# TensorE's step reordered: the transposes of quad 3 and of h ahead of the first feed-forward product, P V ahead of the first values

## What is computed

```python
x = x + tanh(g_xattn) * xattn(layernorm(x), ctx, dist, ...)   # 4 layers
x = x + tanh(g_ffn)   * ffn(layernorm(x), ...)                # 1 layer
# in each layer of xattn, norm(x) = (x - mean) / (std + 1e-6):
q, k, v = norm(x) @ Wq * 64**-0.5, ctx @ Wk, ctx @ Wv         # 16 heads of 64
bias = relu(dist[..., None] @ Wth + bth) @ Wto + bto + mask   # 32 hidden units
w = softmax(q k^T + bias)
x = x + (w v) @ Wo
x = x + relu(norm(x) @ Wf1 + bf1) @ Wf2 + bf2                 # 512 hidden units
```

## Time and profile before

| | us |
|---|---|
| median of 3 runs | 1382.73 |
| lowest, highest | 1380.3, 1384.69 |
| the profiled execution's own time | 1388.81 |
| its span in the profile | 1387.1 |
| PE busy | 1228.3 (89%) |
| DVE busy | 1222.8 (88%) |
| ACT busy | 1064.8 (77%) |
| POOL busy | 834.8 (60%) |

### The profile page before, as it was taken

One profiled execution on the slowest core, in us unless ns is written; L12 is line 12 of the kernel. 1 busy time (PEld: TensorE's weight loads), 2 busy tenths in 40 slices (PEclk: granted clock), 3 DMA queues, 4 the chain that ended last, 5 costly groups with the idle time before them and its releaser, 6 DMA issues.

```text
span 1387.1 us, 39817 instructions
## 1 busy us (share of the span) xinstructions
PE 1228.3 (89%) x11184; PEld 1013.8 (73%) x11184; DVE 1222.8 (88%) x4922; ACT 1064.8 (77%) x3353; POOL 834.8 (60%) x889
## 2 busy tenths in 40 slices
PE   1599989898989899898989898989898999788897
PEld 1377878787878787777878787878787878666665
DVE  4899989898989999898989898989898988579996
ACT  4588878787878888787878686878787876568886
POOL 3677767676767677676767676767676754211110
PEclk9899999999999999999999999999999999989999
DMA  5201000002110000021100101111101000000000
GB/s 153 67 7 30 16 27 12 29 12 76 44 31 12 23 19 22 20 68 34 31 25 13 29 12 31 57 47 28 31 12 42 12 12 9 5 22 19 18 20 9
DMA packets 69117, 41.06 MB, mean 30 GB/s; under 512 B 14841, under 2 KB 63873, under 8 KB 68993
## 3 DMA queue, kind: packets, MB, share of 16 engines
q1 hardware_dynamic: 68992, 39.84, 10.1%
HBM read 23.29 MB, written 1.05 MB: 18 GB/s over the span
## 4 chain that ended last, share of the span: by engine, by line
issue 27%; DVE 24%; ACT 18%; PE 17%; POOL 3%; DVEq 1%; DMA 1%; ACTq 0%; SPq 0%; POOLq 0%
ACT prob L802 10%; DVE bias_acc L951 4%; PE M L582 3%; ACT relu_z L785 3%; PE O L552 3%; DVE score L998 3%; DVE qT L1123 3%; DVE hid L1073 3%; DVE st L1016 2%; PE M L628 2%; PE M L560 2%; PE L L689 1%; ACT probT L809 1%; ACT oT L814 1%; DVE rs L1025 1%
## 5 line engine op out<-in xcount | busy, mean ns | idle before, releaser
L802 ACT ACTIVATE prob<-score,nmax 128x128 f32<-128x128 f32 x1024 | 396.7, 390 | 182.7 <-DVE nmax L998 177.3
L1396 POOL TENSOR_TENSOR prob<-prob,rinv 128x512 f32<-128x512 f32 x256 | 293.9, 1148 | 234.0 <-DVE rinv L1006 231.9
L951 DVE SCALAR_TENSOR_TENSOR bias_acc<-relu_z,cst,bias_acc 128x512 f32<-128x512 f32 x370 | 339.7, 918 | 9.7 <-ACT relu_z L785 0.2
L785 ACT ACTIVATE relu_z<-dist_g,cst 128x512 f32<-128x512 f32 x386 | 294.9, 804 | 16.9 <-DMA cst<-cst_all 16.9
L998 DVE CUSTOM_DVE_ANT_0 score<-L,bias 128x128 f32<-128x128 f32 x1024 | 233.8, 282 | 4.2 <-PE L L528 1.5
L802 ACT ACTIVATION_READ_ACCUMULATOR prob<-score,nmax 128x1 f32 x1024 | 193.2, 189 | 0.0
L1391 POOL TENSOR_TENSOR sd<-mv,half 128x1 f32<-128x1 f32 x128 | 105.6, 825 | 120.4 <-DVE mv L1018 117.6
L538 PE MATMUL T<-ident,prob 128*128 128x128 f32 x1024 | 163.9, 284 | 4.7 <-POOL prob L1396 3.8
L552 PEld LDWEIGHTS O<-probT,v 128*64 128x64 f32 x2048 | 109.3, 136 | 62.0 <-issue 54.4
L582 PE MATMUL M<-wv,ctxT 128*128 128x512 f32 x256 | 147.0, 658 | 7.7 <-DVE hid L1073 5.1
L528 PE MATMUL L<-kT,qT 64*128 64x128 f32 x2048 | 149.6, 286 | 0.0
(11 more groups left out here) (134 smaller groups left out, 2226.7 us busy)
## 6 DMA issues: line engine op xcount, KB each, us to landing
dist_g<-in_fside_BxSxS SPq DMA_DIRECT2D x16, 256.0 KB, 2.7
mask_g<-in_mask_Bx1x1xS_ff SPq DMA_DIRECT2D x16, 256.0 KB, 3.5
ctxT<-ctxT_all SPq DMA_DIRECT2D x64, 64.0 KB, 1.9
xs<-x_all SPq DMA_DIRECT2D x64, 64.0 KB, 1.8
x_all<-xs SPq DMA_DIRECT2D x64, 64.0 KB, 1.9
wk<-in_L_xattn_Wk SPq DMA_DIRECT2D x4, 512.0 KB, 3.7
wv<-in_L_xattn_Wv SPq DMA_DIRECT2D x4, 512.0 KB, 4.3
wq<-in_L_xattn_Wq SPq DMA_DIRECT2D x4, 512.0 KB, 5.0
```

What stands on the lines that cost most here:

```text
L785: nc.scalar.activation(relu_z[:, z_slot(g, k), :], dist_g[:, :, :], ACT.Relu, bias=cst[:, C_BTH + k:C_BTH + k + 1], scale=cst[:, C_WTH + k ...
L802: last = nc.scalar.activation(prob[:, c, m, :], score[:, c, m, :], ACT.Exp, bias=nmax[:, c, m:m + 1], scale=-1.0, accum_out=rsum[:, c, m:m ...
L951: vec.scalar_tensor_tensor(out=bias_acc[:, :], in0=relu_z[:, z_slot(g, k), :], scalar=weight, in1=bias_acc[:, :], op0=ALU.mult, op1=ALU.ad ...
L1396: gp.tensor_tensor(prob[:, c, :, :], prob[:, c, :, :], rinv[:, c, :].rearrange("p (m o) -> p m o", o=1).broadcast_to([P, 4, P]), ALU.mult) ...
```

## The change

Each engine's step is edited where it has to follow PE's new order.

- PE: after the first scores come now the transpose of quad 3 of unit i-1 and the transpose of h of unit i+1, and then the first feed-forward product of unit i-2. Later in the step the second half of P V of unit i-1 comes ahead of the first values product.
- DVE: the copies probT (quad 3) and hT come ahead of the relu hid.
- ACT: the exponentials of quad 1 come ahead of the copy of the first values.
- POOL and SP are not edited. No instruction is added or taken out on any engine.

```diff
@@ PE, step @@
                 if cur:
                     scores(g, i, 0)
+                if prev:
+                    turn(g, i - 1, 3)
+                if nxt:
+                    pe.wait_ge(h_done[0], after(g, i + 1, 1))
+                    wait(pe, h2T_kept, after(g, i - 2, 1))
+                    nc.tensor.transpose(M2[:, 0:P], h[:, (i + 1) % 2, :], ident[:, :]).then_inc(hT_done, 1)
                 if old:
 
                     pe.wait_ge(h2T_kept, after(g, i - 2, 1))
...
                     for c in range(FILT // P):
                         last = mm(M1[:, c * P:(c + 1) * P], wf1[:, c * P:(c + 1) * P], h2T[:, i % 2, :], start=True, stop=True)
                     last.then_inc(f1_done, 1)
-
-                if prev:
-                    turn(g, i - 1, 3)
-                if nxt:
-                    pe.wait_ge(h_done[0], after(g, i + 1, 1))
-                    wait(pe, h2T_kept, after(g, i - 2, 1))
-                    nc.tensor.transpose(M2[:, 0:P], h[:, (i + 1) % 2, :], ident[:, :]).then_inc(hT_done, 1)
+                if nxt:
                     keys(g, i + 1, 1)
+                if prev:
+                    apply(g, i - 1, 1)
+                if nxt:
                     values(g, i + 1, 0)
-                if prev:
-                    apply(g, i - 1, 1)
@@ ACT, step @@
                 relus(g, i, 1)
+                if cur:
+                    exps(g, i, 1)
                 if nxt:
                     act.wait_ge(v_done, after(g, i + 1, 2, 0))
                     wait(act, pv_done, after(g, i - 1, 2, 1))
                     nc.scalar.activation(v[:, (i + 1) % 2, 0:512], M1[:, :], copy).then_inc(v_kept[0], 1)
-                if cur:
-                    exps(g, i, 1)
@@ DVE, step @@
                 if cur:
                     score_quad(g, i, 0)
+                if prev:
+                    keep_turned(g, i - 1, 3)
+                if nxt:
+                    dve.wait_ge(hT_done, after(g, i + 1, 1))
+                    wait(dve, q_done, after(g, i - 1, 2, 1))
+                    vec.tensor_copy(hT[:, (i + 1) % 2, :], M2[:, 0:P]).then_inc(hT_kept, 1)
                 if old:
 
                     for c in range(FILT // P):
...
                     last.then_inc(hid_kept, 1)
-
-                if prev:
-                    keep_turned(g, i - 1, 3)
-                if nxt:
-                    dve.wait_ge(hT_done, after(g, i + 1, 1))
-                    wait(dve, q_done, after(g, i - 1, 2, 1))
-                    vec.tensor_copy(hT[:, (i + 1) % 2, :], M2[:, 0:P]).then_inc(hT_kept, 1)
```

More of the change, by code:

```diff
@@ L629, in step @@
                     last.then_inc(f1_done, 1)
-                if prev:
-                    turn(g, i - 1, 3)
                 if nxt:
-                    pe.wait_ge(h_done[0], after(g, i + 1, 1))
-                    wait(pe, h2T_kept, after(g, i - 2, 1))
-                    nc.tensor.transpose(M2[:, 0:P], h[:, (i + 1) % 2, :], ident[:, :]).then_inc(hT_done, 1)
                     keys(g, i + 1, 1)
-                    values(g, i + 1, 0)
                 if prev:
                     apply(g, i - 1, 1)
+                if nxt:
+                    values(g, i + 1, 0)
                 if old:
```

## The result

| | before | after |
|---|---|---|
| median, us | 1383.71 (4 runs, 1380.3 to 1386.45) | 1403.88 (4 runs, 1402.9 to 1405.4) |
| ratio, 95% interval | 1 | 1.0148 (1.0122 to 1.0174) |
| profiled execution, us | 1388.81 | 1403.04 |
| its span, us | 1387.1 | 1401.2 |

The change makes the kernel 1.5% slower: 20.2 us between the medians, 14.1 between the two spans. None of the other 42 executions of the kernel before, here and beside the experiments, reached 1388.81; the highest took 1387.32. So its one trace shows a slowish execution, and where sums are taken against it the medians stand beside them. What made it slower stays open.

What follows compares the result with a forecast made beforehand. DVE was taken to set the period in steps 1 to 3, its loop turn step 0. 8.8 + 3.3 - 1.5 + 0.9 + 1.3 = +12.8 us took the median 1382.73 to 1395; range 1379 to 1406.

Steps and rivals of the forecast that it cites:

- part 1: PE's transposes of quad 3 and h ahead of the first feed-forward product: PE stands 1.02 us, DVE then waits at hid.
- part 2: P V ahead of the values, exponentials of quad 1 ahead of the copy: no cost, gain only in step 0.
- The wait at hid in steps 1 to 3: DVE waits 0.21 us for the first feed-forward product in each of 42 steps: +8.8 us, ends 4.6 and 17.
- Step 0: Loop's 13 steps 0: DVE 0.87 us late at hid, ACT's earlier work leaves 0.25 each: +3.3 us, ends 0 and 11.3.
- one more long stretch of slow clock: PE's longer idle time in step 0 brings one more long half-clock stretch, as at a layer change: +1.3 us.
- hid would wait some 55 times: Sign expected in the profile after: DVE idle of 0.2 us ahead of hid, released by the first feed-forward product.
- One sign of being wrong: Wrong if hid starts without a wait, steps 1 to 3 shrink, or DVE waits at the sums of Wf2 or Wo.
- rival C: Clearly slower: slow clock prolonged in most groups, or PE's lateness reaches DVE at Wo's sum; 1405 to 1408, chance 0.16.
- The edges: Written-out steps at the end: P V's 1.43 us wait for quad 3's copy goes, 0.5 a step later: -1.5 us.
- the 0.9 us: Three layer changes: the key weights' load is asked for by PE's later keys, 0.3 each: +0.9 us.
- A (ACT's chain is the bound): Faster: what ACT gets early in steps 0 to 2 is kept; 1370, or 1376 with half the wait at hid; chance 0.14.
- B: No change: DVE's wait at hid only 0.05 to 0.1, balanced by step 0 and the end; about 1384, chance 0.20.

Runs made afterwards that it cites:

- the two kernels with one part alone: The kernel before with only the transposes and DVE's copies moved up: 1434.07 us, 1.0362; with only P V's second half and ACT's exponentials moved up: 1384.71 us, 1.0018.
- part 1 alone: The changed kernel with P V put back behind the values and ACT's order as before: 1434.07 us, 1.0362 of the kernel before.

## Why the prediction was right or wrong

The forecast was 1395 us with 1387 to 1402 for its own mechanism and 1379 to 1406 with the rivals; 1403.88 came. The direction and the mechanism of part 1 were right, two sizes were not, and that the time lies inside the wider range owes something to luck.

**The direction and the mechanism of part 1: right.** The prediction had PE stand 1.02 us ahead of the transposes of quad 3, released by POOL, and DVE stand at hid, released by the product. The trace has 0.8 to 1.15 us on PE, less only at the layer changes, and 4.1 to 4.4 in step 0. That the wait lies on the bound is shown by the kernel with DVE's order back and by steps 1 to 3, which grew on DVE's marks by what hid waits there. That part 1 is the cost is shown by the two kernels with one part alone. One reading beside it was wrong: part 2 was said to bring nothing in steps 1 to 3. In the kernel before ACT's edit does leave them as they were, but behind part 1 the whole of part 2 saves 0.67, 0.66 and 0.21 us a step on DVE's marks, since the late hid would otherwise hold ACT.

**The wait at hid in steps 1 to 3: a quarter too large.** The term was 42 x 0.21 = 8.8 us; these steps grew by 6.5 on DVE's marks. In steps 1 and 3 hid waited 0.1 and not 0.21. The place, the start of the product and the copies' 0.80 were as worked out; the product behind the transpose of h is 1.06 long where it was 1.16 behind the scores. A duration was carried from one neighbour to another. In step 2 hid waited 0.25.

**Step 0: the clock was the term sized too small.** I gave step 0 0.25 us and one more long stretch of slow clock, 3.3 + 1.3 = 4.6 us; it measured 9.7 on DVE's marks, 9.3 of them with the clock and 0.4 with the order. What stands behind hid and the copies came 0.96 us later after DVE's first reciprocals than before (789.57 against 784.11, and 778.08 against 773.58: 5.46 against 4.50), for which 0.87 was said. Part 2 was said to give back all but 0.25. It left 0.55: DVE waited 0.22 for the Wo product, and the copy of quad 1 started 13.41 us after the first reciprocals of the step and not 12.86. With the clock held up the 0.96 is 0.02, so this lateness too is the slow clock's. I counted the slow stretch as a cost that both orders pay alike, with one more long one. Four more came, and each order pays by itself: the changed kernel puts quad 3, h and the product one behind the other at the slow clock, and hid waits for the last. The row behind the 1.3 was taken for what a layer change does; of three layer changes one had no long stretch, and the long ones of the changed kernel come in every second group.

**The signs.** I had said that hid would wait some 55 times; the view prints 26, and the waits of 0.1 below it. ACT's copy of the values no longer waits for P V, as said. One sign of being wrong came: in step 0 DVE waits at the sum of Wo, 13 times and 3.1 us. PE's lateness passed DVE's margin, which is the mechanism of rival C, but only there.

**The edges.** The written-out steps at the end gave back 2.6 us on DVE's marks where 1.5 was said: of three waits of P V there, 1.38 to 1.43 us each, one is left, 1.19 us. What I left out is the last group's step 0: with no loop turn behind it PE stood 2.01 us where it stood 1.07, the clock fell to a mean of 0.91, and it took 1.9 us more. I had used its row to show that a gap of a us is safe, and did not ask what 0.9 more would do to it. At the layer changes the 0.9 us did not come: on DVE's marks the steps 2 and 3 there take no longer than elsewhere after the change (16.77 and 18.04), and the three pairs together grew by 0.7 us, less than three ordinary pairs.

**The sum.** 12.8 us were said for the profiled execution and 14.2 came, but that is partly luck, two errors against each other: steps 1 to 3 with the layer changes 3.2 too high (9.7 against 6.5), step 0 5.1 too low (4.6 against 9.7); the edges gave 2.0 back where 1.5 was said. Against the medians 20.2 came. The forecast took 6.1 us off, by which the profiled execution of before lay above its median, as if that of after would lie as far above its own; it lay 0.8 below. This step makes 7.5 of the 8.9 us between 1395 and 1403.88, and no run shows what the 6 us were.

**The rivals.** A (ACT's chain is the bound) has a true core: ACT's edit alone gains 0.28%, and in the kernel with part 1 alone DVE waits for ACT. But what it gains lies in step 0; it had 0.15 us in steps 1 and 2, and there is none. B fell with the periods. C named the clock and the Wo margin, and its price, 1405 to 1408, is nearer to 1403.88 than the forecast's 1395. It had the clock in most groups, and six of 13 were long, and it had the Wo margin in all steps, and it was step 0 alone.

## What to carry to other kernels

Before a transpose is moved up to fill a short gap, look when its operand is ready: a gap of 0.3 us was traded for one of 1.0 because POOL and DVE finish quad 3 and h only then. A step that restarts PE after a long idle time must be costed with every matmul on its path at the slow clock, and a few useless matmuls in the idle time show at once what that clock is worth; here, 0.9% of the kernel before. Count the steps on the engine that sets the period: on PE's marks the gain of ACT's edit seemed to lie in step 1 and most of the order's cost in step 0, and neither does. The order in which a consumer takes its inputs has to follow the producer's: the same PE order with DVE's old order cost 5.0% instead of 1.5%.

## What the runs showed of the hardware

A group of eight matmul records (four products) had two lengths at the same clock: 1.16 us behind the scores and 1.06 behind the transpose of h, both at clock 1.00. The profile models the ends of matmuls, but the starts agree: what follows the product starts 1.00 us after it in the first case (737.01 to 738.01) and 0.90 in the second (804.64 to 805.54). Filling 3.3 us of idle PE in 13 steps of 21.1 us took 1.4 us off each, more than the 0.9 by which the first product got shorter; what else adds to it was not taken apart. In one kernel the stretch of slow clock came out at three sizes (none, short, long) in steps with the same gap, and in all traces the long ones are those in which the clock had fallen 0.6 us or more before PE resumed. In the last group one gap of 2.01 us in a step otherwise busy was followed by a stretch at half clock, and one of 1.07 was not.
